# The layer-0 products of a streamed audio tower: two tiles of a pair side by side on the rows of TensorE's array

## The reference, cut to what matters

```python
CONVS = [(128, 10, 5)] + [(128, 3, 2)] * 4 + [(128, 2, 2)] * 2
...
for w, g, b, s in zip(conv_ws, ln_gs, ln_bs, strides):
    h = _conv1d(h, w, s)
    h = jnp.swapaxes(h, -2, -1)
    h = _fp32_layernorm(h, g, b)
    h = jnp.swapaxes(h, -2, -1)
    h = jax.nn.gelu(h, approximate=False)
```

## Time and profile before

| | |
|---|---|
| median of 3 runs | 2264.59 us (2261.46 to 2267.62) |
| profiled execution, its own time | 2265.01 us |
| its span, first to last instruction | 2263.2 us |
| TensorE busy | 2113.8 us, 93% of the span |
| VectorE, ScalarE, GpSimd busy | 1327.1, 1110.0, 848.9 us |
| L370, the layer-0 product | 376 matmuls, 137.3 us busy |
| L414, its gelu | 376 activations, 286.3 us busy |

### The profile page before, as it was taken

The page is one execution under the profiler, slowest core; times in us unless marked ns, Lnnn a source line. Parts: engine busy times, 40 slices in busy tenths (PEclk is TensorE's granted clock), DMA queues, the critical chain, the costliest instruction groups (busy, mean ns, idle before and its releaser), DMA issues. The chain is left out here.

```text
span 2263.2 us, 40787 instructions
## 1 busy us (share of the span) xinstructions
PE 2113.8 (93%) x14347; PEld 1897.7 (84%) x14347; DVE 1327.1 (59%) x3440; ACT 1110.0 (49%) x2104; POOL 848.9 (38%) x751
## 2 busy tenths in 40 slices
PE   6999999999999999999999989597899799979988
PEld 5889999999999999999999988597856467769978
DVE  5776667667667667667667665242368467632222
ACT  4556555555555565555555554132344367633310
POOL 4445555555565565565455463110142000000000
PEclk9999999999999999999999999699999899989989
DMA  8400000000000000000000020134310011149956
GB/s 270 152 4 4 5 4 4 6 7 4 5 10 4 4 9 4 3 9 4 5 9 4 1 69 1 63 114 133 96 26 16 0 55 55 69 145 326 321 191 210
DMA packets 98641, 137.12 MB, mean 61 GB/s; under 512 B 13811, under 2 KB 79261, under 8 KB 97818
## 3 DMA queue, kind: packets, MB, share of 16 engines
q1 hardware_dynamic: 75146, 105.18, 14.7%
q10 hardware_dynamic: 17744, 20.27, 2.7%
q0 software_dynamic: 5568, 9.27, 1.4%
HBM read 89.14 MB, written 45.50 MB: 59 GB/s over the span
## 5 line engine op out<-in xcount | busy, mean ns | idle before, releaser
L506 POOL TENSOR_TENSOR t_rstd<-t_var,t_minus_half 128x4 f32<-128x4 f32 (+1 forms) x379 | 367.0, 968 | 630.3 <-DVE t_var L426 628.8
L317 PE MATMUL banks<-t_wt,t_l 128*128 128x256 f32 (+1 forms) x2836 | 595.9, 349 | 0.0
L317 PEld LDWEIGHTS banks<-t_wt,t_l 128*128 128x128 f32 x2836 | 509.0, 192 | 51.6
L380 ACT ACTIVATE t_sq<-banks 128x512 f32<-128x512 f32 (+1 forms) x379 | 215.9, 570 | 567.1 <-PE banks L317 565.7
L434 DVE TENSOR_TENSOR t_yn<-banks,t_rstd 128x512 f32<-128x512 f32 (+1 forms) x379 | 248.8, 656 | 368.0 <-POOL t_rstd L506 366.4
L308 PE MATMUL banks<-t_wt,t_l 128*128 128x128 f32 x2836 | 386.5, 278 | 4.3 <-ACT t_l L398 2.9
L308 PEld LDWEIGHTS banks<-t_wt,t_l 128*128 128x128 f32 x2836 | 356.1, 194 | 14.4 <-ACT t_l L398 3.9
L512 POOL TENSOR_TENSOR t_zrstd<-t_zvar,t_minus_half 128x8 f32<-128x8 f32 x188 | 307.6, 1637 | 12.2 <-DVE t_zvar L470 12.2
L414 ACT ACTIVATE t_l<-banks,t_cols 128x512 f32<-128x512 f32 x376 | 286.3, 777 | 27.9 <-PE banks L370 24.4
L398 ACT ACTIVATE t_l<-banks,t_cols 128x512 f32<-128x512 f32 (+1 forms) x381 | 284.8, 747 | 12.0 <-PE banks L330 6.8
L423 DVE TENSOR_REDUCE t_ss<-t_sq 128x4 f32<-128x512 f32 (+1 forms) x379 | 244.5, 645 | 75.9 <-ACT t_sq L380 69.0
(11 more groups left out here) (374 smaller groups left out, 3310.8 us busy)
## 6 DMA issues: line engine op xcount, KB each, us to landing
t_w<-in_w SPq DMA_DIRECT2D x64, 480.0 KB
ect<-t_ECT SPq DMA_DIRECT2D x16, 750.0 KB, 3.2
t_l<-in_w1a SPq DMA_DIRECT2D x27, 384.0 KB, 3.7
sorted_by_expert<-t_h SPq DMA_DIRECT2D x4, 2400.0 KB, 11.6
routed_by_expert<-t_h SPq DMA_DIRECT2D x4, 2400.0 KB, 18.3
t_ectb<-ect ACTq DMA_DIRECT2D x5, 1500.0 KB, 7.8
t_w1x<-in_w1x SPq DMA_DIRECT2D x64, 97.5 KB
ys<-t_ye ACTq DMA_DIRECT2D x64, 96.0 KB
```

What stands on the lines that cost most here:

```text
L317: mm = pe.matmul(psY[bank][:, t * C:end * C], src[:, at:at + P], weights[:, C:(1 + end - t) * C], start=False, stop=(t + 1 == n))
L380: act.activation(T["sq"][:, par, 0:n], psY[bank][:, 0:n], ACT.Square).then_inc(S["squared"], 1)
L506: pool.tensor_tensor(T["rstd"][:, par, 0:n], T["var"][:, par, 0:n], T["minus_half"][:, 0:n], ALU.pow)\
```

## The change

Each slot's half of a pair now stands in its own 64 rows. `p60` gets 64 instead of 60 entries for each position, the last four zero, so that a transpose of two positions puts slot 0 in rows 0 to 63 and slot 1 in rows 64 to 127. The weights `w60` are one set of 64 rows, written twice, in rows 0 to 59 and 64 to 123, with zeros between. `layer0_pair` issues both matmuls of a pair one behind the other, each over 64 rows of the array (`tile_position` 0 and 64) and each into its own bank. The compiled program has 188 matmuls of 64 x 128 at position 0 and 188 at position 64, where 376 of 128 x 128 stood; all other matmuls of the stream keep 128 x 128.

The tables move with it. `L0_BEHIND` is gone, and the pairs stand in the middle of g = 5, 6, 7. ScalarE has tables of its own, `GELU0_MIDDLE` and `GELU0_BEHIND`. A pair waits until both tiles of the pair before it have been read.

```diff
@@ -54,9 +55,11 @@
 LAG = 2
 
 
-L0_MIDDLE = {5: (3,), 6: (5,), 7: (7,)}
-L0_BEHIND = {4: (2,), 5: (4,), 6: (6,)}
+
+L0_MIDDLE = {5: (2, 3), 6: (4, 5), 7: (6, 7)}
 L0_END = {3: (0, 1)}
+GELU0_MIDDLE = {5: (2,), 6: (4,), 7: (6, 7)}
+GELU0_BEHIND = {5: (3,), 6: (5,)}
 INPUT_OF = {1: 0, 2: 1, 3: 2, 4: 3}
 
 
@@ -218,11 +223,8 @@
 
             pe.wait_ge(S["w0_split"], 1)
             pe.wait_ge(S["pick_ready"], PARTS)
-            for slot in range(2):
-                at = ROWS * (1 - slot)
-                for part in range(3):
-                    mm = pe.matmul(w60[:, slot * C:(slot + 1) * C], T["pick"][:, part, at:at + 2 * ROWS], T["w0parts"][:, part, :],
-                                   start=(part == 0), stop=(part == 2))
+            for part in range(3):
+                mm = pe.matmul(w60, T["pick"][:, part, :], T["w0parts"][:, part, :], start=(part == 0), stop=(part == 2))
             mm.then_inc(S["w60_done"], 1)
 
         @block.scalar
@@ -231,14 +233,15 @@
             act.activation(T["identb"][:, :], T["ident"][:, :], ACT.Copy)
             act.wait_ge(S["pool_zero"], 1)
             for n, (_, part) in enumerate(SPLIT):
-                r = ROWS + n * TAPS0
+                r = n * TAPS0
                 act.activation(T["pick"][:, part, r:r + TAPS0], T["ident"][0:TAPS0, 0:TAPS0], ACT.Copy)\
                     .then_inc(S["pick_ready"], 1)
             for flat in (T["l2"][:, :], T["l3"][:, :], T["yn"][:, :, :].rearrange("p a n -> p (a n)")):
                 zeros = bcast(T["minus_half"][:, 0], flat.shape[1])
                 act.activation(flat, zeros, ACT.Identity, scale=0.0)
             act.wait_ge(S["w60_done"], 1)
-            act.activation(T["w60"][:, :, :].rearrange("r s c -> r (s c)"), w60, ACT.Copy)
+            for side in range(2):
+                act.activation(T["w60"][SIDE * side:SIDE * side + ROWS, :], w60, ACT.Copy)
 
 
 def x_chunk(io, c):
@@ -293,8 +296,8 @@
         products(pe, event(j, g), lambda: layer0s(pe, j + 1, L0_MIDDLE.get(g, ())))
 
     def layer0s(pe, c, tiles):
-        for i in tiles if c < CHUNKS else ():
-            layer0(pe, c, i)
+        for i in tiles[::2] if c < CHUNKS else ():
+            layer0_pair(pe, c, i)
 
     def products(pe, e, in_the_middle=None):
         layer, half, bank, _, _, _ = e
@@ -339,7 +342,7 @@
             pe.wait_ge(S["patch_copied"], 2 * c + 1)
         for n in range(8):
             q = 8 * half + n
-            mm = pe.transpose(psPb[0:2 * ROWS, n * P:(n + 1) * P],
+            mm = pe.transpose(psPb[:, n * P:(n + 1) * P],
                               p60[:, 2 * q:2 * q + 2, :].rearrange("p a r -> p (a r)"), T["identb"][:, :])
         mm.then_inc(S["patch_turned"], 1)
 
@@ -361,15 +364,16 @@
                            T["band"][0:WINH, :], start=True, stop=True)
         mm.then_inc(S["gram_applied"], 1)
 
-    def layer0(pe, c, i):
+    def layer0_pair(pe, c, i):
         if i % 4 == 0:
             pe.wait_ge(S["patch_copied"], 2 * c + i // 4 + 1)
-        if not isinstance(c, int) or 8 * c + i >= 2:
-            pe.wait_ge(S["l0_ready"], 8 * c + i - 1)
-        q, slot = i // 2, i % 2
-        pe.matmul(psL[i % 2][:, :], T["w60"][:, slot, :],
-                  p60T[:, 4 * q:4 * q + 4, :].rearrange("r a p -> r (a p)"),
-                  start=True, stop=True).then_inc(S["l0_done"], 1)
+        if 8 * c + i >= 2:
+            pe.wait_ge(S["l0_ready"], 8 * c + i)
+        q = i // 2
+        for side in range(2):
+            r = slice(SIDE * side, SIDE * (side + 1))
+            pe.matmul(psL[side][:, :], T["w60"][r, :], p60T[r, 4 * q:4 * q + 4, :].rearrange("r a p -> r (a p)"),
+                      start=True, stop=True, tile_position=(SIDE * side, 0)).then_inc(S["l0_done"], 1)
 
 
     def square(act, e):
@@ -402,7 +406,7 @@
         return tiles if j + 1 < CHUNKS else ()
 
     def gelu0(act, c, i):
-        act.wait_ge(S["l0_done"], 8 * c + i + 1)
+        act.wait_ge(S["l0_done"], 8 * c + 2 * (i // 2) + 2)
         if i == 6:
             last = block_at(0, POS - 2)
             act.wait_ge(S["l0_ready"], 8 * c + i)
@@ -448,7 +452,7 @@
         dve.wait_ge(S["patch_turned"], 2 * c + half + 1)
         if not (isinstance(c, int) and c == 0):
             dve.wait_ge(S["l0_done"], 8 * c)
-        dve.tensor_copy(p60T[:, 8 * half:8 * half + 8, :].rearrange("r a p -> r (a p)"), psPb[0:2 * ROWS, :])\
+        dve.tensor_copy(p60T[:, 8 * half:8 * half + 8, :].rearrange("r a p -> r (a p)"), psPb[:, :])\
             .then_inc(S["patch_copied"], 1)
 
     def copy_windows(dve, c):
@@ -1353,7 +1357,6 @@
             for j in range(CHUNKS):
                 for g in range(NG):
                     conv(pe, j, g)
-                    layer0s(pe, j + 1, L0_BEHIND.get(g, ()))
                     transposes(pe, event(j if g >= LAG else j - 1, (g - LAG) % NG))
                     if g == 5 and j + 3 < CHUNKS:
                         window_transposes(pe, j + 3)
@@ -1392,10 +1395,10 @@
                 gelu0(act, 0, i)
             for j in range(CHUNKS):
                 for g in range(NG):
-                    for i in ahead(j, L0_MIDDLE.get(g, ())):
+                    for i in ahead(j, GELU0_MIDDLE.get(g, ())):
                         gelu0(act, j + 1, i)
                     square(act, event(j, g))
-                    for i in ahead(j, L0_BEHIND.get(g, ())):
+                    for i in ahead(j, GELU0_BEHIND.get(g, ())):
                         gelu0(act, j + 1, i)
                     back = 0 if g >= LAG else 1
 
@@ -2618,9 +2621,9 @@
                         sl("w0c", [P, TAPS0])
                         n = STRIDE0 * (HALF - 1) + WINH
                         T["gram"] = T["late"][0:TAPS0, 0:n]
-                        T["pick"] = T["late"][0:TAPS0, n:n + 9 * ROWS // 2].bitcast(BF16).rearrange("t (n r) -> t n r", n=3)
+                        T["pick"] = T["late"][0:TAPS0, n:n + 3 * ROWS // 2].bitcast(BF16).rearrange("t (n r) -> t n r", n=3)
                         sl("band", [WINH, HALF * TAPS0])
-                        sl("w60", [2 * ROWS, 2, C], BF16)
+                        sl("w60", [P, C], BF16)
                         sl("xs", [P, XS_RING, WIN])
                         sl("xT", [WINH, 2, P])
                         sl("zz", [P, POS, TAPS0])
@@ -2629,8 +2632,8 @@
                         sl("zrstd", [P, POS])
                         sl("scaled", [P, POS, TAPS0])
                         sl("rest", [P, POS, TAPS0])
-                        sl("p60", [P, POS, ROWS], BF16)
-                        sl("p60T", [2 * ROWS, PAIRS, P], BF16)
+                        sl("p60", [P, POS, SIDE], BF16)
+                        sl("p60T", [P, PAIRS, P], BF16)
                         sl("l0", [P, BLOCK * BLOCKS[0]])
                         sl("l1", [P, BLOCK * BLOCKS[1]])
 
```

More of the change, by code:

```diff
@@ L31 @@
 ROWS = PARTS * TAPS0
+SIDE = P // 2
 PHI = (("phA", P), ("phB", P))
@@ L131, in setup @@
 def setup(nc, T, S, io):
-    band, w60 = T["psL"][0][0:WINH, 0:HALF * TAPS0], T["psL"][1][0:2 * ROWS, 0:2 * C]
+    band, w60 = T["psL"][0][0:WINH, 0:HALF * TAPS0], T["psL"][1][0:ROWS, 0:C]
     middle = STRIDE0 * (HALF - 1)
@@ L160, in _ @@
             pool.memset(T["pick"][:, :, :], 0.0)
+            pool.memset(T["w60"][:, :], 0.0)
             pool.memset(T["minus_half"][:, :], -0.5)
             pool.memset(T["gram"][:, :], 0.0).then_inc(S["pool_zero"], 1)
+            pool.memset(T["p60"][:, :, ROWS:SIDE], 0.0)
             pool.memset(T["one"][:, :], 1.0).then_inc(S["one_ready"], 1)
```

## The result

The changed kernel took 2276.63 us (median of 5 runs, 2273.52 to 2279.63), the kernel before 2263.7 us (5 runs, 2261.46 to 2267.62). The ratio is 1.0053, with a 95% interval of 1.0041 to 1.0065. The forecast was 2242 us and faster; the time lies within the range given, on its slow side.

The account below looks back on a forecast made before the run. TensorE's stream of matmuls was taken to bound the kernel. Overlap -40.5, wait +11.1 and switches +6.8 gave -22.6 us, from 2265.01 to 2242 us, 1.0% faster; range 2234 to 2291 us.

Parts of the forecast that it names:

- What bounds the kernel: Whole stream: TensorE's matmuls set the time, busy 93% of the span; other engines have a third or more to spare.
- A pair overlaps: Layer-0 pairs in the stream: both matmuls run together, 0.22 us instead of 0.44, 184 pairs, 40.5 us saved.
- The new order makes a wait: Pair (6,7), middle of g = 7: TensorE waits 0.41 us for tile 5's gelu in 27 chunks, 11.1 us added.
- It fits by 0.03, so I take 0: Pair (4,5), g = 6: tile 3's gelu needs 1.53 us, TensorE's path 1.56, so no wait was counted.
- The switch between shapes: Around each pair: going to the half shape and back costs 0.02 us a switch, 341 on the path, 6.8 us added.
- The break-even: All switches on the path: at 0.086 us a switch the pairs' saving is used up and the change gains nothing.
- A pair has two weight loads as before ... so I put nothing on it: At each pair: two weight loads as before, 0.10 us each, counted as no extra time.
- the right rival: At each switch TensorE runs empty: 0.16 us each, 54.6 us in all, 2290 us and slower; chance 0.27.
- The sum: Whole kernel: -40.5 + 11.1 + 6.8 = -22.6 us, giving 2242 us, 1.0% faster.

Follow-up runs that it names:

- the extra pass: The changed kernel with each pair's two matmuls issued twice in a row, the second pass overwriting the first: 2309.99 us, ratio 1.0185 to the kernel before.
- the order alone: The changed kernel with its order, layout and waits, but every layer-0 product over all 128 rows: 2273.63 us, ratio 1.0039 to the kernel before.
- bf16 behind one pair: The changed kernel with pair (0,1) moved ahead of the second half of the patch transposes at g = 3: 2277.26 us, ratio 1.0038 to the kernel before.

## Why the prediction was wrong, step by step

- **What bounds the kernel** held in plain chunks: what TensorE's stream gains or loses, the chunk does, to 0.01 us. In the chunks with a chain's steps it did not; there VectorE has a say. I had read the waits of TensorE as next to none. But a row shows a wait only beyond the modelled end of the matmul ahead, 0.16 us later, so the nineteenth chunk's waits of 0.17, 0.23 and 0.29 us were in no row, and of the 0.74 there it shows 0.58.
- **A pair overlaps** and saves 0.22: right. Two rows within 0.01 us; the extra pass costs 0.215. The page TensorE: Matmul & The Clock Gate (the Trainium skill, "Measured speedup vs the span model") has some 4 ns for the further tile; the trace agrees, with 3 to 5 ns between the two starts in all 188 pairs.
- **The new order makes a wait**: right in place, size and kind (0.41 forecast, 0.40 measured; 27 entries of L375). The size of the order alone was forecast at 11.1 us and measured at 9.7 (2273.63 - 2263.91). "It fits by 0.03, so I take 0" for pair (4,5) was wrong by 0.05 or 0.06 us in that run; in the changed kernel this hides under the gap.
- **The switch between shapes** is the step that failed: "The nearest rows are other changes of shape ... I take 0.02 for a switch". Changes of type and of transposing had no price in the earlier trace rows, and from them nothing follows for a change of the array's rows. (Elsewhere one does cost, in the kernel before too: the first float32 record of g = 3, behind eight bf16 transposes, takes 0.16 us and not 0.11, at 241.11 in the eighth chunk.) It measured 0.09 or 0.10 each way, plus 0.11 for float32 weights behind it, about 0.30 for a pair instead of 0.04, and so more than the 0.22 that the pair saves. The pairs were to win 40.5 - 6.8 = 33.7 us and cost some 3 beyond the order alone. The break-even I had worked out, 0.086 us a switch, was passed already by the two gaps.
- **"A pair has two weight loads as before ... so I put nothing on it"** failed with it. The page TensorEngine Tiling (Array Packing) (the Trainium skill, "Key Properties") says that a change of mode drains the engine. The gaps of 0.09 to 0.10 us around each pair agree with it, though no row shows the array empty. The rule was the right rival, and I priced it from the tail of a matmul, 0.16, where a gap took 0.10. The load of 0.11 behind the pair, which the rule does not mention, made up for the difference.
- **The sum** by the measured terms, for a plain chunk: the order +0.45, four pairs at +0.08 = 0.32, less the gaps ahead of two pairs that hide in their waits, 0.09 + 0.05 = 0.14, gives 0.63; measured 0.64. Over 46 chunks that would be 29 us; the stream took 15.9, with the 1.6 of the clock in it, because the chunks with a chain did not pay it, and the kernel 12.9. So the time fell into the range by luck: 29 us would have made 2293, outside it, and that the chunks with a chain take up half of that was in no term.
- **The 4.6 us behind the stream** stay open, and may be no effect at all. From its end (1417.2 and 1433.0) to the end of the span the profiled execution before took 846.1 us and that of the changed kernel 841.5, the shortest of the twelve kernels' traces, which have 841.5 to 847.8 (845.2 with the order alone, 844.5 with bf16 behind one pair). They come back in the experts' stage: its first product started 16.6 us later than before (2022.3 to 2038.9), its last 12.5 us later (2176.0 to 2188.5).

## What to carry to other kernels

Two half-height matmuls side by side save one stream of the array, but going into the half shape and out of it costs two gaps and the hidden weight load. With 0.22 us saved and 0.3 us paid, one pair between full-shape matmuls loses; two pairs back to back would have paid by an estimate from the run with each pair twice (0.22 + 0.53 = 0.75 against 0.88), if there were banks for them. Price a change of the array's shape from a row that has one, or by an eight-column matmul put in for the purpose; the changes of type beside it say nothing. And before work is moved away from between a result and the next matmul that needs its bank, look what it had covered: here the gelu of tile 5 went behind a square, while tile 6's product, 0.22 us, left TensorE's way to the pair that waits for that gelu. The order alone made 9.7 of the 12.9 us.

## What the runs showed that I had not expected

- In the rows read here no weights load ahead across a change of shape, though they do across the changes of type: a load starts with its own matmul, at 815.72 and 816.04. What that costs goes with the length of the load: 0.01 us for bf16 (0.10), 0.05 for the float32 transposes (0.14), 0.11 for a convolution's float32 weights (0.19).
- Without any switch a load can be too late as well: behind bf16 transposes of 128 columns the first float32 record takes 0.16 us instead of 0.11.
- A single matmul of 64 rows costs as much as a pair between full-shape matmuls (0.32 to the next start in both), and one of 64 rows and 8 columns still costs 0.21.
- Added time can vanish: 0.85 us more in a plain chunk went with 0.44 us less in a chunk with a chain (30.92 to 30.48).
- Two executions whose mean clock agrees still differ in short stretches of 3.4 us at the lower level, at 1.4 to 1.7 us each; such a stretch looks like a slower chunk.
